# Branch condition loaded once a batch, and other hand-written step orders on five engines, in a 32-batch conditional transformer stack

## The chip, the cores and the metric

The program runs on one core of one Trainium2 chip. The metric is the device time of that core in microseconds (us) for the whole batch of 32 sequences; lower is better.

## What is computed

Each of 32 batch entries is a 256 x 256 matrix of float32 (256 tokens, width 256). It passes four layers.

```python
x = rotate(x, theta[b], phi[b])                      # pairs of columns turned by an angle
h = gelu(x @ Wi[e] + bi[e]); o = h @ Wo[e] + bo[e]   # e = expert of this batch entry, width 1024
x = layernorm(o + x) * gamma[e] + beta[e]
# one of three branches, by c = itok_B_0_2[b]
c == 0: out = gelu(x @ w1_nr + b1) @ w2_nr + b2
c == 1: out = gelu(x @ w1_tsr + b1) @ w2_tsr + b2
c == 2: out = gelu(gelu(x @ w1_sr + b1) @ w2_sr + b2) @ w3_sr + b3      # w1_sr is 256 x 512
x = layernorm(x + out) * gamma + beta
x = layernorm(x) * (1 + scale[b]) + shift[b]          # from a time step
p = softmax(q k^T / 4 + bias[b] + mask[b])            # 16 heads of 16, bias is 16 x 256 x 256 per entry
x = x + (p v) @ Wo
x = x + gelu2(layernorm(x) @ W1) @ W2                 # width 1024
```

In the data of this case c is 0 in 12 of the 32 entries, 1 in 10 and 2 in 10 (entries 2, 4, 8, 10, 11, 15, 17, 18, 27 and 30).

## The kernel before

The kernel is written engine by engine. Each engine has one instruction stream in program order, and the streams meet only through semaphores (`wait_ge`, `then_inc`). The work of a batch entry b is cut into four streams of steps:

- wide, letter g: rotation and expert layer. On TensorE (PE) its steps are the transposes of the input ("turnx0"), wide_in 0 to 3 and wide_out 0 to 3; on VectorE (DVE) `rotate`, then the sum with its statistics, then the scaling of layer 1, called scale1 below; on ScalarE (ACT) the copy of x0 and four gelus.
- front, letter f: the branch, the second and third normalisation, q, k and v. On PE: transposes of y1 ("turny1"), branch_in, branch_middle, branch_out, transposes of x2, q, k, v. On DVE the first step makes x1's low part (xa_lo); scale3 is the third scaling (it makes x2). On ACT the first step makes x1's high part (xa_hi), the second ("br_a") the gelu of the branch, the third seeds PSUM with the branch's bias row ("seedF"), the fourth ("br_b") is the second gelu of c == 2 and only a semaphore step otherwise.
- attention, letter h: for each head h of 16, PE has scores S(h) (a mask matmul and two score matmuls) and T(h) (four transposes of the shifted scores), after every fourth head the values V and the context transposes C (V1 and C1 come with heads 8 and 9, V2 and C2 with heads 12 and 13, V3 and C3 with heads 0 and 1 of the next entry). DVE has the maxima M(h): two additions of the bias with a row maximum, two subtractions. ACT has the exponential E(h). T(h) waits for M(h)'s subtractions and for E(h-1), since there is one PSUM bank of transposed scores; S(h+1) waits for M(h)'s additions.
- tail, letter r: output projection and the feed-forward layer. On PE: transposes, wo, transposes, then the halves "hidden" 0 to 3 (h0 to h3) and "narrowed" 0 to 3 (n0 to n3), 12 matmuls each. On ACT seed, tanh and high for each m2; on DVE x3lo (the low part of the layer's input), gate g0 to g3 and low l0 to l3.

Matrices are split in a high and a low part, so that a product of 256 x 256 is 12 matmuls; branch_in and branch_middle have 24 for c == 2.

The order in which an engine takes the steps of the four streams is a hand-written string of letters: `FIRST[engine] + ORDER[engine] * 25 + LAST[engine]`, where each letter takes the next step of that stream. `ORDER` is one batch entry's worth of steps (68 letters on PE, 48 on ACT, 46 on DVE, 7 on GpSimd, 27 on the DMA queue of SyncE). The streams are offset against each other: while the attention of entry b runs its second half, front works on entry b+2 and wide on entry b+3.

Three places on PE (L597, L608, L619), two on ACT (L847, L859) and two on DVE (L1133, L1141) read the entry's condition c from SBUF into a register with `value_load` and branch on it with `e.If`. In branch_in the load stands behind the wait for `x1_hi`, in branch_out behind the wait for `branch_seeded`, in ACT's br_a behind the waits for `dma_spill`, `wide_out`. The waits for buffers: br_a writes `hid`, which the previous entry's q and k spills (DMAs out of `hid`) must have left.

SyncE issues every DMA in one order. A bias block for head h+7 waits for T(h); the fetch of expert weights (raw0 to raw3) waits for wide_out 0 to 3; the load of the next x waits for scale1's first half; out waits for the end of the tail; the spills wait for q's and k's low parts; st0 and st1 bring the spilled q and k back as stacks. DVE's scale3 waits for the out DMA of two entries earlier (`dma_out`), since `res` has three buffers.

Of the kernel before, what the change touches and what calls it, by code (L numbers as in the profile page):

```python
# [43 lines left out]
    "DVE": (
        "gggffffffgffffghhhghhfhfhghhfhhfhffhhfhfhfhfggfhhfhgfhfhffhfhrhhrfrhfrfhhghrhghrrfhhhrhrfhgfhhrr"
        "hfrhhfhhrrfrhrhrfghfrg"),
    "POOL": "ggffggfffgfggffrrfgfrgfgfr",
    "SP": "gggggfffggfhgghghhhhhhfhghhghfgfgfghhfhhhfhhhhghgffghhhfhgghhfhhhrhfghhhgghhggh",
}
ORDER = {  # L50
    "PE": "hhfhhfhhhhfrrhhfrhhfhhhghhhghhrhhghhhhhhgrgrhhgghhrgghhrfhhhhfrrhhfr",
    "ACT": "rhrhrfhrrhfrrrhfrhfrfhhfhrffrhfhhrhghhghhhgrhghg",
    "DVE": "hrhfrhrfhrhfhhrfhrfhghrhhhrhhfhfrhrhrfhrfghrfg",
    "POOL": "frgrfgf",
    "SP": "hfhfhhfhhhhffggrhhhhhhghghg",
# [3 lines left out]
        "hhhhhhhhfhhrhhrhhhhfhhfrhhfhhgfhhhghhhgrhhrgrghhgrhhhfghrfhhgfhhhhghhfhrfhhhfhhfrfghhrghhhrhhhrg"  # L59
        "rhhghhghhhrhhhrghrhgfghhrfhhhhhhrfhhghhfhhhhhhrrrhhffhhhhrhhhhrhhhhffhhhhhhrhhrrhhhhrhhhhfrhhfhh"  # L60
        "rhhhhhhrfhhrhhrhhhhhhfrhhrhhrhhhhhhrrhhhhrhhhhhhrhhhhrhhhhhhrrhhrhhrhhhhhhrhhrhhhhhhhhhhrrrhhrhr"
        "hhhhrhhhhhrhhhrhrhrhhhhhhhhrhhhhhhr"),
# [4 lines left out]
    "DVE": (
        "hrhfrhhrhfhhrhrhhgfhhrfhhffhfrhhfrhrrrhfrhfhfhhfrhghgrfhhrfghfhrrfhhrhhrhrhfrhhfrfrhrfhrhfhhhfhr"
        "hgrhrhghfrhrhfhhhfrhrfhfhhrhfhrrhrfrhhfrhhrhfrhhrhfhrhhhrhrhrhrhhrhrhrhhrhrhhrhrhhrhrrhhrhhrhhhr"
        "hhrhrrrhhhhrhhhrhrrrhrrhrrrhhhhh"),  # L70
    "POOL": "fgfrrggfffrfgrffrfrrrrr",
# [1301 lines left out]
```

## Time and profile before

| | us |
|---|---|
| median of 3 runs | 2076.05 (2075.35 to 2077.53) |
| span of the profiled execution | 2069.5 |
| PE busy | 1921.3 (93%) |
| weight loads of PE busy | 1676.1 (81%) |
| DVE busy | 1590.7 (77%) |
| ACT busy | 1376.7 (67%) |
| GpSimd busy | 252.4 (12%) |
| DMA, mean over the span | 172 GB/s |

The span goes from the first to the last instruction of one profiled execution. The profile gives no device time of that execution beside it; the median lies 6.55 us above the span. Busy is the time in which an instruction of the engine runs. A matmul's record of 0.28 us starts every 0.12 us when PE runs without a break, so records overlap, and an idle time counts from the end of the last record.

### The profile page before, as it was taken

How to read it: one execution, taken by the hardware profiler on the slowest of the kernel's cores; microseconds unless marked ns; L12 is line 12 of the kernel's file. 1: busy time of each engine (PE TensorE's matmuls, PEld its weight loads, DVE VectorE, ACT ScalarE, POOL GpSimd, SP SyncE). 2: the span in 40 equal slices, each digit the busy share in tenths (PEclk: the TensorE clock that was granted, in tenths of full speed). 3: DMA queues.
4: the chain of work that ended last, by engine and by line, in shares of the span. 5: the costliest groups of instructions: out<-in, count | busy, mean ns of one | idle time of the engine just before them, and what ended most of it. 6: DMA issues, size and time to landing. Idle time of an engine off the chain costs nothing.

```text
span 2069.5 us, 43614 instructions
## 1 busy us (share of the span) xinstructions
PE 1921.3 (93%) x14354; PEld 1676.1 (81%) x14354; DVE 1590.7 (77%) x5373; ACT 1376.7 (67%) x2210; POOL 252.4 (12%) x361
## 2 busy tenths in 40 slices
PE   5789999999999999999999999999999999999786
PEld 4668888888888888888888888888888888788676
DVE  4577877787887788887777888778888877877774
ACT  3376677677667677767767767766776776666443
POOL 1111111011111011111001111101111110111100
PEclk9799999999999999999999999999999999999998
DMA  6655555665565566654555655556665546653450
GB/s 221 202 172 167 187 153 158 186 203 182 183 178 148 156 202 192 196 181 154 154 187 183 195 172 179 164 174 201 189 196 181 177 146 177 216 159 118 133 153 11
DMA packets 222311, 356.12 MB, mean 172 GB/s; under 512 B 29523, under 2 KB 120147, under 8 KB 222068
## 3 DMA queue, kind: packets, MB, share of 16 engines
q1 hardware_dynamic: 222068, 352.99, 56.0%
q8 instruction: 139, 2.28, 0.5%
q14 instruction: 104, 0.85, 0.1%
HBM read 294.12 MB, written 58.79 MB: 171 GB/s over the span
## 4 chain that ended last, share of the span: by engine, by line
PE 76%; DVE 12%; issue 5%; ACT 4%; DMA 1%; ACTq 0%; SPq 0%; POOL 0%; DVEq 0%; POOLq 0%
PE pD L471 51%; PE pX L687 11%; PE pS L471 9%; DVE bias_ring L1178 4%; PE pC L471 3%; DVE bias_ring L975 3%; PE pC L709 1%; DVE x_nat L972 1%; ACT L777 1%; DVE crossed L972 1%; ACT gelu_out L777 1%; ACT probs L777 1%; ACT hid L777 1%; DVE res L978 0%; DVE y_nat L978 0%
## 5 line engine op out<-in xcount | busy, mean ns | idle before, releaser
L1178 DVE CUSTOM_DVE_ANT_0 bias_ring<-pS,bias_ring 128x256 f32<-128x256 f32 x1024 | 389.5, 418 | 200.3 <-PE pS L471 197.4
L777 ACT ACTIVATE probs<-pX 128x512 f32<-128x512 f32 x512 | 304.6, 595 | 225.1 <-PE pX L687 222.8
L777 ACT ACT_TABLE_LOAD x341 | 437.5, 1283 | 18.9 <-PE pD L471 12.0
L687 PE MATMUL pX<-ident,bias_ring 128*128 128x128 f32 x2048 | 321.2, 280 | 61.4 <-DVE bias_ring L975 49.3
L687 PEld LDWEIGHTS pX<-ident,bias_ring 128*128 128x128 f32 x2048 | 228.9, 141 | 147.2 <-issue 95.9
L975 DVE TENSOR_SCALAR bias_ring<-bias_ring,row_max 128x256 f32<-128x256 f32 x1024 | 321.8, 357 | 18.3
L471 PE MATMUL pS<-k_stack,q_stack 96*128 96x256 f32 x1024 | 304.5, 379 | 0.0
L471 PE MATMUL pD<-x,raw 128*128 128x256 f32 x1024 | 246.4, 384 | 3.0 <-ACT gelu_out L777 1.0
L471 PE MATMUL pD<-raw,gelu_out 128*128 128x256 f32 x1024 | 237.6, 379 | 0.0
L471 PEld LDWEIGHTS pS<-k_stack,q_stack 96*128 96x128 f32 x1024 | 197.9, 193 | 19.8
L471 PEld LDWEIGHTS pD<-x,raw 128*128 128x128 f32 x1024 | 188.2, 191 | 31.8 <-issue 9.7
L471 PE MATMUL pD<-w_hi,ffn 128*128 128x256 f32 x1024 | 206.3, 284 | 0.6 <-ACT ffn L777 0.6
L471 PEld LDWEIGHTS pD<-raw,gelu_out 128*128 128x128 f32 x1024 | 187.3, 190 | 22.2 <-issue 0.4
L471 PE MATMUL pS<-mask_add,eye_bf 128*128 128x512 bf16 x512 | 196.0, 383 | 0.9 <-DMA k_stack<-k_spill 0.9
L471 PEld LDWEIGHTS pD<-w_hi,ffn 128*128 128x128 f32 x1024 | 168.5, 191 | 1.8 <-issue 0.8
L1264 POOL TENSOR_SCALAR front_var_eps<-front_mean_var 128x2 f32<-128x2 f32 x64 | 13.3, 207 | 1240.8 <-DVE front_mean_var L1059 1198.1
L777 ACT ACTIVATE gated<-pD 128x512 f32<-128x512 f32 x128 | 76.4, 597 | 109.0 <-PE pD L471 109.0
L777 ACT ACTIVATE gelu_out<-pD,chosen 128x256 f32<-128x256 f32 x300 | 126.0, 471 | 33.4 <-PE pD L471 31.8
L471 PE MATMUL pD<-xc_hi,w_hi 128*128 128x256 f32 x512 | 131.6, 289 | 6.1 <-ACT pD L777 6.1
L471 PE MATMUL pC<-probs,v_aug 128*17 128x256 f32 x2048 | 135.4, 382 | 0.7 <-issue 0.7
L471 PE MATMUL pD<-xc_hi,w_lo 128*128 128x256 f32 x512 | 130.0, 286 | 0.0
L471 PE MATMUL pD<-w_lo,ffn 128*128 128x256 f32 x512 | 128.4, 283 | 0.0
(148 smaller groups left out, 3663.4 us busy)
## 6 DMA issues: line engine op xcount, KB each, us to landing
bias_ring<-in_fside SPq DMA_DIRECT2D x512, 256.0 KB, 4.4
raw<-in_experts SPq DMA_DIRECT2D x128, 512.0 KB, 4.7
q_spill<-hid SPq DMA_DIRECT2D x96, 256.0 KB, 3.4
k_spill<-hid SPq DMA_DIRECT2D x96, 256.0 KB, 3.4
q_stack<-q_spill SPq DMA_DIRECT2D x128, 192.0 KB, 4.3
k_stack<-k_spill SPq DMA_DIRECT2D x64, 384.0 KB, 5.6
norm<-in_expert_rows SPq DMA_DIRECT2D x32, 384.0 KB, 4.1
x_nat<-in_x SPq DMA_DIRECT2D x32, 256.0 KB, 3.1
```

The source lines that it names most:

```text
L471: return e.matmul(o, lhsT, rhs, start=start, stop=stop, skip_group_check=True, **kw)
L687: last = e.transpose(pX[:, k, t * P:(t + 1) * P], bias_ring[:, u % NBIAS, t, k * P:(k + 1) * P], ident[:, :])
L709: last = e.transpose(pC[:, 1, t * P:(t + 1) * P], ctx_raw[:, t * P:(t + 1) * P], ident[:, :])
L777: return e.activation(o, i, func, bias=bias, scale=scale)
L972: return e.tensor_tensor(o, a, c, op)
L975: return e.tensor_scalar(o, a, s1, None, op0) if op1 is None else e.tensor_scalar(o, a, s1, s2, op0, op1)
L1178: e.tensor_tensor_reduce(bias_ring[:, n, t, :], pS[:, t, :], bias_ring[:, n, t, :], 1.0, -3.4e38, ALU.add, ALU.max, row_max[:, n, t:t + 1] ...
L1264: e.tensor_scalar(var_eps[which][:, :], mean_var[which][:, :, 1], eps, 1.0, ALU.add, ALU.mult).then_inc(sem[which + "_eps"], 1)
```

## The change

The condition is loaded once at the start of the front stream's first step of a batch entry on PE, ACT and DVE, in front of that step's waits, and the register serves all branches of that entry. The waits that stood ahead of the branches now stand inside each arm. The three strings of every engine are replaced.

In the cyclic part this makes the following moves. PE: V1 goes in front of turny1; n1 goes from behind branch_in to between T9 and S10, so that the order is T8 S9 V1 turny1 T9 n1 S10 C1 branch_in h3 T10 S11 branch_middle n2 T11 S12 branch_out (before: T8 S9 turny1 V1 T9 S10 C1 branch_in n1 h3 T10 S11 branch_middle n2 T11 S12 branch_out). The rest of PE's cycle is as before. ACT: E6 in front of seed2 and high1, mask in front of seed3, tanh3 and E10 in front of seedF, C2's copy in front of high3. DVE: rotate goes from between M12 and M13 to between M9 and xa_lo, l2 in front of M10, g3 from behind M11 to between M12 and M13, klo in front of l1, l0 in front of the normalising of context 0, scale3 in front of x3lo. GpSimd: the root of the third normalisation (root3) goes in front of two additions, of which one comes last now. SyncE: st0 one bias block later, st1 two earlier, then raw0, out, block 14, raw1, block 15, raw2, block 0, raw3, x and norm1, blocks 1 and 2, q spill (before: raw0, raw1, out, blocks 14 to 3, raw2, block 4, raw3, block 5, x and norm1, block 6, q spill); so blocks 3 to 7 come between the q spill and the k spill, where before only block 7 did. Block h here is the one that waits for T(h). FIRST and LAST hold the same moves for the entries at the ends and some swaps of neighbours.

```diff
--- before.py
+++ after.py
...
 ORDER = {
-    "PE": "hhfhhfhhhhfrrhhfrhhfhhhghhhghhrhhghhhhhhgrgrhhgghhrgghhrfhhhhfrrhhfr",
-    "ACT": "rhrhrfhrrhfrrrhfrhfrfhhfhrffrhfhhrhghhghhhgrhghg",
-    "DVE": "hrhfrhrfhrhfhhrfhrfhghrhhhrhhfhfrhrhrfhrfghrfg",
-    "POOL": "frgrfgf",
-    "SP": "hfhfhhfhhhhffggrhhhhhhghghg",
+    "PE": "fhhhfhrhhfrhhfrhhfhhhghhhghhrhhghhhhhhgrgrhhgghhrgghhrfhhhhfrrhhfrhh",
+    "ACT": "fhrrhfrhrrfrhffrhhfhrfrhffhhhrghhghhhgrhghgrhrhr",
+    "DVE": "frhfrhrhgfhrhfhfhrhrhhhrhhfhfrhrhrfhfrghrfgrhh",
+    "POOL": "frfggfr",
+    "SP": "hfhhhfhfhfhgrhghghgghhfhhhh",
 }
...
@@ -592,20 +592,20 @@
             def front(b):
                 def branch_in():
                     xa = [(xa_hi[:, k, :], xa_lo[:, k, :]) for k in range(K)]
-                    low = sem["x1_lo"], b + 1
-                    e.wait_ge(sem["x1_hi"], b + 1)
-                    c = e.value_load(idx[0:1, 1, b:b + 1])
+                    high, low = (sem["x1_hi"], b + 1), (sem["x1_lo"], b + 1)
                     with e.If(c == 2):
+                        e.wait_ge(*high)
                         for i in range(2):
                             to_turned(BANK[f"deep{i}"], "w1_sr", SR, 2 * P * i, xa, low).then_inc(sem["pe_deep"], 1)
                     with e.Else():
                         with e.If(c == 1):
+                            e.wait_ge(*high)
                             to_turned(BANK["narrow"], "w1_tsr", H, 0, xa, low).then_inc(sem["pe_narrow"], 1)
                         with e.Else():
+                            e.wait_ge(*high)
                             to_turned(BANK["narrow"], "w1_nr", H, 0, xa, low).then_inc(sem["pe_narrow"], 1)
 
                 def branch_middle():
-                    c = e.value_load(idx[0:1, 1, b:b + 1])
                     with e.If(c == 2):
                         e.wait_ge(sem["dve_deep"], 3 * b + 2)
                         ins = [(hid[:, s, 0, n, :], hid[:, s, 1, n, :]) for s in range(2) for n in range(2)]
@@ -615,20 +615,26 @@
 
                 def branch_out():
                     ins = [(hid[:, 0, 0, n, :], hid[:, 0, 1, n, :]) for n in range(2)]
-                    e.wait_ge(sem["branch_seeded"], b + 1)
-                    c = e.value_load(idx[0:1, 1, b:b + 1])
+
+                    def narrow_ready():
+                        e.wait_ge(sem["branch_seeded"], b + 1)
+                        e.wait_ge(sem["act_narrow"], 3 * b + 3)
+                        e.wait_ge(sem["dve_narrow"], b + 1)
+
                     with e.If(c == 2):
+                        e.wait_ge(sem["branch_seeded"], b + 1)
                         e.wait_ge(sem["act_deep"], 9 * b + 9)
                         to_natural(SUM_F, "w3_sr", 0, ins, (sem["dve_deep"], 3 * b + 3), start=False).then_inc(sem["branch_done"], 1)
                         e.sem_inc(sem["pe_narrow"], 1)
                     with e.Else():
-                        e.wait_ge(sem["act_narrow"], 3 * b + 3)
-                        e.wait_ge(sem["dve_narrow"], b + 1)
                         with e.If(c == 1):
+                            narrow_ready()
                             to_natural(SUM_F, "w2_tsr", 0, ins, start=False).then_inc(sem["branch_done"], 1)
                         with e.Else():
+                            narrow_ready()
                             to_natural(SUM_F, "w2_nr", 0, ins, start=False).then_inc(sem["branch_done"], 1)
 
+                c = e.value_load(idx[0:1, 1, b:b + 1])
                 if b:
                     e.wait_ge(sem["v_made"], 2 * b)
                 e.wait_ge(sem["y1_made"], b + 1)
@@ -834,21 +840,25 @@
                     e.wait_ge(sem["pe_deep"], 3 * b + i + 1)
                     gelu_and_hi(BANK[f"deep{i}"], i % 2, i % 2, [col(name, first + n) for n in range(2)], "act_deep", 9 * b + 3 * i)
 
+                c = e.value_load(idx[0:1, 1, b:b + 1])
                 e.wait_ge(sem["y1_turned"], b + 1)
                 if b:
                     e.wait_ge(sem["branch_done"], b)
                 act(flat(xa_hi[:, :, :]), flat(pD[:, BANK["y1"], :, :]), ACT.Copy).then_inc(sem["x1_hi"], 1)
                 yield
-                if b:
-                    e.wait_ge(sem["dma_spill"], 96 * b)
-                e.wait_ge(sem["wide_out"], 4 * b + 4)
-                if not b:
-                    e.wait_ge(sem["dve_cols"], 1)
-                c = e.value_load(idx[0:1, 1, b:b + 1])
+                def hid_free():
+                    if b:
+                        e.wait_ge(sem["dma_spill"], 96 * b)
+                    e.wait_ge(sem["wide_out"], 4 * b + 4)
+                    if not b:
+                        e.wait_ge(sem["dve_cols"], 1)
+
                 with e.If(c == 2):
+                    hid_free()
                     deep(0)
                     deep(1)
                 with e.Else():
+                    hid_free()
                     narrow()
                 yield
 
@@ -856,7 +866,6 @@
                 e.wait_ge(sem["dma_brow"], 16 * (b + 1))
                 act(pD[:, SUM_F, :, :], branch_row[:, :].unsqueeze(1).to_broadcast([P, T, H]), ACT.Copy).then_inc(sem["branch_seeded"], 1)
                 yield
-                c = e.value_load(idx[0:1, 1, b:b + 1])
                 with e.If(c == 2):
                     e.wait_ge(sem["dve_deep"], 3 * b + 1)
                     deep(2)
@@ -1119,6 +1128,7 @@
                 yield
 
             def front(b):
+                c = e.value_load(idx[0:1, 1, b:b + 1])
                 e.wait_ge(sem["x1_hi"], b + 1)
                 low_of(xa_hi[:, :, :], xa_lo[:, :, :], flat(pD[:, BANK["y1"], :, :])).then_inc(sem["x1_lo"], 1)
                 yield
@@ -1130,7 +1140,6 @@
                     e.wait_ge(sem["act_deep"], 9 * b + 3 * i + 3)
                     low_part(i % 2, i % 2, "dve_deep")
 
-                c = e.value_load(idx[0:1, 1, b:b + 1])
                 with e.If(c == 2):
                     deep(0)
                     deep(1)
@@ -1138,7 +1147,6 @@
                     e.wait_ge(sem["act_narrow"], 3 * b + 3)
                     low_part(0, 0, "dve_narrow")
                 yield
-                c = e.value_load(idx[0:1, 1, b:b + 1])
                 with e.If(c == 2):
                     deep(2)
                     e.sem_inc(sem["dve_narrow"], 1)
```

The changed strings of FIRST and LAST are left out where the diff shows "...".

## Rows read from the trace of the kernel before

**Rows 1.** The page: DMA issues, KB each, median us from issue to landing.

```profile
bias_ring<-in_fside SPq DMA_DIRECT2D x512, 256.0 KB, 4.4
```

**Rows 2.** Busy time by stretch: start, middle, end, one cycle (stretch, length, busy).

```profile
0.00:277.70 277.70, 228.67 (x1493) 195.59 (x1493) 181.49 (x563) 156.99 (x254) 33.79 (x50) 0.93 0.61 185
277.70:1739.90 1462.20, 1411.41 (x10716) 1235.64 (x10716) 1172.59 (x3999) 1042.25 (x1658) 185.80 (x264) 1.00 0.59 179
1739.90:2069.50 329.60, 281.26 (x2146) 244.83 (x2146) 236.60 (x813) 177.44 (x300) 32.83 (x47) 0.96 0.43 130
827.40:886.90 59.50, 57.46 (x437) 50.30 (x438) 48.52 (x168) 42.27 (x68) 7.74 (x11) 1.00 0.61 184
```

**Rows 3.** Waits of PE: line, waited for; total us, times, longest.

```profile
PE pX L687 <- DVE bias_ring L975: 49.3, 85, 2.1
PE pD L471 <- DVE x_nat L972: 20.3, 20, 13.3
PE pD L471 <- issue: 18.4, 31, 4.1
```

**Rows 4.** Chain that ended last, in order of time: start, us, what.

```profile
813.74 0.59 issue
814.33 4.58 PE pD L471 x36
```

**Rows 5.** Lines 597 and 598 on PE's sequencer: ns min/median/max.

```profile
L597 PEldq TENSOR_LOAD <-idx x32: 296/302/497, 38.3 to 1918.8; - x32
L598 PEldq COMPARE_BRANCH  x42: 68/207/361, 38.8 to 1919.2; - x42
```

**Rows 6.** Timeline of ACT, 812.8 to 819 us: start, us, instruction, [idle before].

```profile
812.82 0.59 ACT L777 ACTIVATE xa_hi<-pD 128x512 fp32r<-128x512 f32 x1
...
814.43 1.28 ACT L777 ACT_TABLE_LOAD   x1
...
818.93 0.60 ACT L777 ACTIVATE gated<-pD 128x512 f32<-128x512 f32 x1 [0.89 <-PE pD L471]
```

**Rows 7.** Timeline of PE: the breaks at T11, turnx0, T13; branch_out of a c == 2.

```profile
821.49 0.66 PE L687 MATMUL pX<-ident,bias_ring 128*128 128x128 f32 x4 [0.28 <-ACT probs L777]
826.34 0.63 PE L471 MATMUL pD<-ident,x_nat 128*128 128x128 f32 x4 [0.17 <-DVE x_nat L972]
827.42 0.63 PE L687 MATMUL pX<-ident,bias_ring 128*128 128x128 f32 x4 [0.45 <-DVE bias_ring L975]
...
1069.38 0.39 PE L471 MATMUL pD<-w_hi,hid 128*128 128x256 f32 x1 [0.60 <-ACT hid L777]
```

**Rows 8.** Timeline of DVE: xa_lo, the rotation's first and last instruction.

```profile
813.44 0.69 DVE L972 TENSOR_TENSOR xa_lo<-pD,xa_hi 128x512 fp32r<-128x512 f32 x1 [0.93 <-ACT xa_hi L777]
...
823.98 0.76 DVE L972 TENSOR_TENSOR crossed<-x_nat,rot_sin 128x256 f32<-128x256 f32 x2
...
825.50 0.69 DVE L972 TENSOR_TENSOR x_nat<-x_nat,crossed 128x512 f32<-128x512 f32 x1
```

**Rows 9.** Timeline of DVE: x3lo, scale3 behind it, and M8.

```profile
851.86 0.68 DVE L972 TENSOR_TENSOR xc_lo<-pD,xc_hi 128x512 fp32r<-128x512 f32 x1
852.78 0.88 DVE L978 SCALAR_TENSOR_TENSOR res<-y_nat,front_mean_var,norm 128x256 f32<-128x256 f32 x2 [0.23 <-issue]
...
868.22 0.42 DVE L1178 CUSTOM_DVE_ANT_0 bias_ring<-pS,bias_ring 128x256 f32<-128x256 f32 x1 [0.44 <-PE pS L471]
```

**Rows 10.** Timeline of PE: the first matmul of h0.

```profile
854.90 0.28 PE L471 MATMUL pD<-xc_hi,w_hi 128*128 128x256 f32 x1
```

**Rows 11.** DMA issues on SyncE's queue: k spills, the next stack load, norm1.

```profile
808.58 1.54 SPq L294 DMA_DIRECT2D k_spill<-hid  x3
...
813.52 0.86 SPq L294 DMA_DIRECT2D q_stack<-q_spill  x2
...
860.69 0.34 SPq L294 DMA_DIRECT2D norm<-in_expert_rows  x1
```

**Rows 12.** DMA view, 840 to 904 us in 40 slices: GB/s moved.

```profile
GB/s 0 13 271 47 0 72 255 392 403 408 401 351 188 259 159 41 326 291 216 342 149 149 360 239 128 161 56 108 164 0 159 5 67 258 257 117 13 0 0 238
```

More of the change, by code:

```diff
@@ L37 @@
     "PE": (
-        "gggggggggffffgffgfgfgggggghhhhhhfhhhhhfhhhfhhhghhfhhghhhghhhgghhfgfhhgghhfghfhhfhfhhfhhfghhhghhh"
-        "ggfrghhghhrghhfrgfhhhhgrhhfhhrhhhfhhhfrhhrhhrhhhfhhhrgfhhgrhhghhhghhhrrghrhgghhrgghhrfhhhhfrrhhf"
-        "r"),
+        "gggggggggffffgffgfggggfggghhhhhhfhhhhhfhhhfhhhghhfhhghhhghhhgghhfgfhhgghhfghhfhfhfhhfhhfghhhghhh"
+        "ggfrghhghhrghhhfrgfhhhgrhhfhhrhhhfhhhfrhhrhhrhhfhhhhrgfhhghrhghhhghhhrrghrhgghhrgghhrfhhhhfrrhhf"
+        "rhh"),
     "ACT": (
-        "gggggffffgffgfgggffhhhhfhffhhfhghhghhghhfgfhghfhfhfffhffhghhgghrhgfhgfrhrfhhrhfrhrrfhhfhrfhrfhrh"
-        "hrfrhrghrghghhhrhgg"),
+        "gggggffffgffgfgggffhhhhfhffhhfhghhghhghfhgfhghfhffhffhffhghhgghrhgfhgfrhfhrhhrfrhrhfrfhhrfhrfhrr"
+        "fhhrhrghrghhghhrhggrhrhr"),
     "DVE": (
[L45 to L48, printed above, removed]
+        "gggffffffgffffghhhghhfhfhghfhhhfhffhhfhfhfhfgghfhfhgfhffhfhfhhrhrfrfrhfhhghrhghrrfhhhrhrfhgfhhrr"
+        "hfhrhfhhrfrrhrhrfghfrgrhh"),
+    "POOL": "ggfffggfffggffrgfgrfrgffgr",
+    "SP": "gggggffgfgghfhghghhhfhghhfhgfgghhhfghhfhfhhhhhhgghfgfgghfhhhhfhhrhhhfhghgghhgghhf",
 }
 ORDER = {
-    "PE": "hhfhhfhhhhfrrhhfrhhfhhhghhhghhrhhghhhhhhgrgrhhgghhrgghhrfhhhhfrrhhfr",
-    "ACT": "rhrhrfhrrhfrrrhfrhfrfhhfhrffrhfhhrhghhghhhgrhghg",
-    "DVE": "hrhfrhrfhrhfhhrfhrfhghrhhhrhhfhfrhrhrfhrfghrfg",
-    "POOL": "frgrfgf",
-    "SP": "hfhfhhfhhhhffggrhhhhhhghghg",
+    "PE": "fhhhfhrhhfrhhfrhhfhhhghhhghhrhhghhhhhhgrgrhhgghhrgghhrfhhhhfrrhhfrhh",
[3 more added lines that the diff above has]
+    "SP": "hfhhhfhfhfhgrhghghgghhfhhhh",
 }
@@ L58 @@
     "PE": (
[L59 to L62, printed above, removed]
+        "hhhhhhfhhrhhrhhhhfhhfrhhfhhgfhhhghhhrghhrgrghhgrhhhfghrfhhgfhhhhghhfhrfhhhfhhfrfghhrghhhrhhrhgrh"
+        "hghhghhhrhhhrhrghgfghhrfhhhhhhrfhhghhfhhhhhhrrrhhffhhhhhrhhhrhhhhffhhhhhhrhhrhhrhhrhhhhfrhhfhhrh"
+        "hhhhhrfhhrhhrhhhhhhfrhhrhhrhhhhhhrrhhhhrhhhhhhrhhhhrhhhhhhrrhhrhhrhhhhhhrhhrhhhhhhhrhrhhhrrhrhhr"
+        "hhhhhhhhhhhrrhrhrhhhhhhhhrhhhhhhr"),
     "ACT": (
-        "rhrrhfhrrfrhrrhhhfhrhrhfrhfhhrhffhffhrghhghgrhhghrhrfhrfghfrhrfhfhrfhfrffhgrhrhgrhhrgrhrhhghhrhf"
-        "hrfhrhghfhrhrhhrffrhrrfrhhfhrhhfhrfhrhrhhhrhhhfhrhrhfrhhrrhrfrhhrhrhhfrfhrhrhrhhhrhhhhrrhhrhrrhh"
-        "rrhrrrhrhhhrhhhrhhhrrrhhhrrrrrhhrhrhhrhhhhrrhhrhh"),
+        "fhrrfrhrrhhhfhhrrhfrhfhhrfhfffhrhghhghrghghhrhrfhrfghfhrrffhrhfhfrfrfhghrhgrhhrrghhrhghhrhfhrfhr"
+        "hghfhrhhrhrhffrrrfrhhfhrhfhhrhfrrhhhhhrhhfhrhrhrfhhrrhrrfhhrhrhhffrrhhrhrhhhrhhhhrhrhrhrrhhrrhrr"
+        "rhrhhhrhhhrhrhrhhhrhrrrhrrhrrhrhhrhhhrrhhhhh"),
     "DVE": (
[L68 to L71, printed above, removed]
+        "frhhrhfhhrhhrhgfhhrfhfhfhfrhhfrhrrrhfrhffhhrhfhghgrfhhrfghfhrhrfhrhhrhrhfrhhfrfrhrfhrhfhhhfhrhgh"
+        "rrhghfrhrhfhhhrfhfrhfhhrhfhrrhrfrhhfrhhrhfrhhrhfhrhhhrhrhrhrhhrhrhrhhrhrhhrhrhhrhrrhhrhhrhhhrhrh"
+        "rhrrhhrrhhhhhrhhrrrrhrrrhhhhh"),
+    "POOL": "gffrgfgrffrrfgffrrrrfrr",
     "SP": (
-        "hfhhfhhhhfhfhhfhhghrhhghgfhfhghghfhffhhhhrhhhhffhhhhhhhhhhffhfhhrghhhhhhhhgffhfhhhhfhhghhhhghhhh"
-        "hhhhhhhhhhhhhhrfrhhhhhhhhhrghh"),
+        "hhfhfhhhhhfhfhrhhhhghghfhgfhgghfhffhhhhrhhhhhhffhhhhhfhhhfhhhfhrghhhhhhhgffhfhhfhhhghhhhhghhhhhh"
+        "hhhhhhhhhhhhrfrhhhhhhhrhhghh"),
 }
```

## The prediction

> **What bounds the kernel now.** I read the busy times by stretch first. In the middle, where the cycle of orders runs, PE is busy 1411.41 of 1462.20 us; in the first 277.7 us and the last 329.6 us it idles 49.0 and 48.3 us [rows 2]. One cycle of a c below 2 is 59.50 us with PE busy 57.46, DVE 48.52, ACT 42.27 and DMA at 0.61 [rows 2]. So PE bounds the cycle, at full clock (1.00), and only what closes a break on PE can shorten it. The reader is to see how little there is: 2.04 us a cycle. The waits of PE then say who makes the breaks: the subtractions of DVE 49.3 us, the rotated x_nat 20.3 us (13.3 of it once, at the start), and 18.4 us of "issue", 31 times, once an entry [rows 3]. The chain of waits shows the last kind in front of branch_in: 0.59 us in which nothing but PE's own sequencer is late, then 36 matmuls in 4.58 us, which is 1.5 us for each group of 12 [rows 4].
>
> PE's records overlap when it runs unbroken: 0.28 us each, one every 0.12 us. A break of r us in the records therefore costs about r + 0.14 us. That is 0.73 in front of branch_in, 0.42 at T11, 0.31 at turnx0, 0.59 at T13 [rows 4, 7].
>
> **The change, part by part (a cycle with c below 2).**
>
> Load of c, and branch_in. Before, xa_hi is written until 812.82 + 0.59 = 813.41; only then does the sequencer load c (0.30 us) and branch (0.07 to 0.36 us), and the first matmul starts at 813.74 + 0.59 = 814.33 [rows 4 to 6]. So 0.92 us pass between the data and the work. After, n1 (1.44 us at 0.12 a matmul), S10 and C1 lie between turny1 and branch_in. xa_hi needs turny1, ACT's copy of context 1, and its own 0.59 us, so by my count it is there about 1 us before branch_in's turn; the branches run while PE works off what is queued. I leave 0.1 us of the 0.73. Gain 0.63. n1's cover is not lost elsewhere: it is the same work in another place, and l1 and high1, which it needs, come before M9 and E7 in both orders. The load itself (0.30) moves to turny1, behind V1's matmuls (about 1 us of work); if that cover went, it would cost its 0.30.
>
> T11. It waits for E10, E10 for a table load of 1.28 us behind tanh3, and tanh3 for h3 [rows 6, 7]. Between h3 and T11 PE does T10, S11, n2 in both orders, and tanh3 starts right behind h3 in both. The 0.42 stays; gain 0. br_a's gelus and copy and h3 (1.44) now run side by side and end together, which may push tanh3 by 0 to 0.1. SeedF, a copy of xa_hi's size (0.59 us), now stands behind E10 and holds the table load of E11 back by that much; by my count E11 ends at T12's turn, so the cost is between 0 and 0.3; I take 0 to 0.1.
>
> turnx0 and T13. The rotation is 825.50 + 0.69 - 823.98 = 2.21 us on DVE [rows 8]. It stood between M12 and M13: turnx0 waited for it, and T13 for M13 behind it [rows 7]. Now it stands behind M9, where DVE idled 0.93 us [rows 8], and only g3 precedes M13, 0.68 us as x3lo, which has its size [rows 9]. x is there: its load goes out ahead of norm1's at 860.69 [rows 11], and M9 follows M8 of 868.22 [rows 9]. M13 then starts when S13 is done, and V2 and turnx0 cover its two additions of 0.42 us [rows 9] and the first subtraction. Gain 0.31 + 0.59 = 0.9, of which 0 to 0.1 may stay at T13. What is late next: xa_lo comes 1.3 us later against xa_hi, but branch_in needs it only after 8 of its matmuls (0.96 us) and starts later against turny1 by n1; by the rows 0.6 us are to spare. M10, with l2 (0.7, again of x3lo's size) now ahead of it, has 0.3 us to spare before T10. If both were gone, each 0.1 us more would be 0.1 us a cycle.
>
> scale3 in front of x3lo. x3lo ran 851.86 to 852.54, and scale3 started at 852.78 [rows 9]; its wait for the out DMA ended then, since out was issued behind raw1. After, out is issued some 5 us earlier and scale3 starts at once. x3lo gets 1.8 us later (scale3 1.80), to about 854.2; seed0 (0.60) follows, to 854.9, and h0's turn is at 854.90 [rows 10]. Cost 0.1 (0 to 0.4).
>
> DVE's, ACT's and GpSimd's other swaps (klo and l1, E6 and seed2, mask and seed3, l0, root3, C2's copy and high3) move steps of under 1.5 us inside stretches in which PE waits for none of them: 0.
>
> Sum: 0.63 + 0.9 = 1.53 without any cost, and 1.53 - 0.1 (T13) - 0.1 (T12) - 0.1 (h0) = 1.23 with them. I take 1.35: the 0.1 at h0 I count, of the other two half.
>
> A cycle with c == 2: the break in front of branch_in is only 0.2 in the records, turnx0 and T13 are as above, and branch_out's 0.60 stays, because it hangs on the end of branch_middle, a table load and a gelu in both orders [rows 7]. Gain 0.25 + 1.0 - 0.1 = 1.15.
>
> Places: the new order holds for the front steps of entries 4 to 28, 17 of them with c below 2 and 8 with c == 2: 17 x 1.35 + 8 x 1.15 = 32. In a third of the entries the branch takes the long 0.33 us instead of 0.2 [rows 5]; that goes too: 2. Ends: 97 us of idle [rows 2], of which the swaps touch little; some branch_in breaks there go too. I take 3, between -4 and 8. Total 37 us: 2069.5 becomes 2032.5 in the profiled execution, and with the 6.55 us that the median stands above the span, 2039.
>
> **SyncE's queue and the DMAs.** Before, the k spills are issued from 808.58 and have landed by 813.52, when the stack load that waits for them goes out [rows 11]. br_a waits for them too, and its table load of 1.28 us comes behind that wait; the table load started at 814.43, high2 and not the spill deciding [rows 6]. After, blocks 3 to 7 (5 x 256 KB) stand between q and k spill. Issue takes 0.5 us each and fits into the time up to k's low part; on the DMA engines, 1.3 MB at 400 GB/s, which the DMA view shows where blocks follow each other [rows 12], is 3.3 us, of which about 2.5 falls into idle time of the engines or the wait for k. branch_in ends 0.7 us later against k's step than before, so the spill may land 1.2 us later and cost nothing. I take 0.
>
> The Trainium skill, DMA: Bandwidth & Descriptors (Queues, rings and completion order), says that each DMA engine takes the descriptors of a ring in ring order, so the spill would stand behind all five blocks; taken alone it speaks for the second rival below.
>
> **The rivals.**
> - The sequencer stays exposed. The gain at branch_in is only the load, 0.37 us, and a first branch of 0.2 to 0.36 still shows [rows 5]. For it: the branch decides what is fetched next, so nothing of the arm can be queued before. Against: in c == 2 the load and a 0.07 us branch leave 0.2. Loses 0.35 x 25 = 9: 2048. The Trainium skill, Runtime: NRT & Kernel Launch (Instruction fetch mechanics), says that a taken branch out of the fetched window stalls on a fetch; that speaks for this rival.
> - The k spill lands late, more than 1.2 us behind its time: at 2.2 us more, branch_a's gelu, tanh3, E10 and T11 shift by 1 us. 25 x 1 = 25: 2064.
> - Slower: x and norm1 now stand ahead of block 1 and wait for scale1; norm1 goes out at 860.69, block 1 at about 861.2, and M8 starts at 868.22 [rows 9, 11]. Landing takes 4.4 us as a median [rows 1], so 2.6 of 7.0 us are free. Above 7.0 + 1.35 = 8.35 us the lateness outweighs the gain. At 9.5 us: (2.5 - 1.35) x 25 = 29 more, less the 5 of the ends and long branches: 2100. It decides from a mean landing of twice the median.
> - The gains of one break are eaten by the next (xa_lo behind the rotation, M10, E11): DVE has 0.3 us to spare at M10; 1.3 us lost there a cycle gives about 2073.
>
> **How the numbers follow.** Forecast 0.55 (own range 2028 to 2050), exposed sequencer 0.17, late spill 0.15, gains eaten 0.07, slower 0.06. All of the cycle's breaks but T11 gone and 8 us at the ends would be 2028; the late spill is the upper end, 2064. That leaves 0.13 above and little below. A measurement of this kernel tells 0.2% (4 us) from no change. Faster by more: 0.88; within: 0.06; slower: 0.06.
>
> **What would show it.** Right: PE's waits lose x_nat (20.3 to about 14, the start's 13.3 staying) and most of "issue"; DVE's subtractions fall from 49.3 by 25 x 0.45 = 11; the cycle is 58.1 us for c below 2; the 0.28 at T11 and 0.60 at branch_out stay. Exposed sequencer: "issue" still 0.2 or more in front of branch_in. Late spill: ACT's table load of br_a starts behind the spill, and T11's break grows. Slower: M(8) or M(9) waits for bias_ring from DMA. The prediction is wrong if DVE or ACT becomes continuous between T8 and T13, or if the ends grow.

## The result and the profile after

The changed kernel takes 2112.0 us (median, 2108.5 to 2117.0) against 2075.35 us of the kernel before on the same chip: ratio 1.0185, 95% interval 1.0170 to 1.0199 (as recorded for all runs; the two medians alone would give 1.0177). It is slower by 1.9%, where 2039 was forecast. The profiled execution spans 2110.3 us, 40.8 more than before; the medians differ by 36.7. The table below splits the 40.8 of these two executions, so a place in it can be off by a few us: the runs of the kernel before lie between 2070.6 and 2077.5.

The longest waits of PE in the changed kernel (what PE waited for, us in total, times, longest one), to be held against [rows 3]:

```profile
engine line waited for: us in total, times, longest us
PE pX L693 <- ACT probs L783: 39.0, 27, 3.5
PE pX L693 <- DVE bias_ring L984: 35.4, 61, 1.4
PE pD L471 <- ACT pD L783: 22.7, 32, 3.1
PE pD L471 <- DVE hid L981: 15.9, 10, 2.7
PE pD L471 <- DVE x_nat L981: 13.6, 2, 13.3
PE pD L471 <- ACT hid L783: 7.6, 10, 1.8
PE pD L471 <- DVE ffn_in L1086: 5.3, 3, 3.7
PE pS L471 <- DMA k_stack<-k_spill: 5.0, 1, 5.0
PE pD L471 <- issue: 5.0, 15, 0.5
```

What the change was to remove did go: "issue" (PE waits for nothing that the profile shows) 18.4 to 5.0, the rotated x_nat 20.3 to 13.6, the subtractions of DVE 49.3 to 35.4 (11 was forecast, 14 came). Of the 15 "issue" breaks 14 stand in front of turny1, behind the moved load of c, and none in front of branch_in. In place of what went stand waits for ACT, for the exponentials (probs) and for the seed of the tail's bank (pD), and 5 us once for the k stack.

To see where they fall I measured the cycle from start to start of PE's steps (first weight load of each, in one traced execution of each kernel): means over the 17 entries with c below 2 among the entries 5 to 28 of the front stream, in us. The last three rows are sums over all entries. "All four" is the best kernel of the experiments below; each column right of it has one of its four edits undone.

| c below 2 | before | changed | all four | waits in arms | GpSimd | x3lo | SyncE |
|---|---|---|---|---|---|---|---|
| T8 to branch_in | 4.37 | 5.22 | 4.97 | 4.98 | 4.98 | 4.98 | 5.04 |
| branch_in to T11 | 7.17 | 7.05 | 5.74 | **7.05** | 5.73 | 5.74 | **6.08** |
| T11 to T13 | 5.89 | 4.87 | 4.86 | 4.86 | 4.86 | 4.86 | 4.87 |
| T13 to T4 | 26.41 | 26.44 | 26.44 | 26.44 | 26.44 | 26.44 | 26.44 |
| T4 to T5 (h0) | 4.05 | 4.82 | 4.11 | 4.11 | 4.12 | **5.25** | 4.09 |
| T5 to T6 | 5.46 | 5.72 | 5.43 | 5.46 | **6.33** | 5.38 | 5.41 |
| T6 to T8 | 6.24 | 6.33 | 6.24 | 6.24 | **6.33** | 6.24 | 6.24 |
| cycle | 59.59 | 60.45 | 57.79 | 59.14 | 58.79 | 58.89 | 58.17 |
| start, up to T8 of entry 2 | 255.5 | 267.0 | 253.3 | 262.2 | 258.8 | 255.5 | 264.0 |
| 24 cycles | 1467.0 | 1492.4 | 1429.5 | 1461.3 | 1453.1 | 1456.1 | 1435.9 |
| end | 347.0 | 350.9 | 343.5 | 351.7 | 347.4 | 345.0 | 345.1 |

So of the 40.8 us, 11.5 are lost in the start, 25.4 in the 24 cycles and 3.9 at the end. In the cycle the move of n1 puts 1.44 us of work ahead of branch_in and takes it from branch_in to T11, so 7.17 ought to become 5.73; it is 7.05. That is the largest loss, and h0 (0.77) and T6 (0.26) are the others. The rotation's gain, T11 to T13, is there in full (1.02).

ACT and PE at that place in the changed kernel, entry 14 of the front stream, c = 0 (start, duration, what; in brackets the idle time before it and what ended it), to be held against [rows 6, 7]:

```profile
898.46 1.28 ACT L783 ACT_TABLE_LOAD   x1 [2.24 <-PE pD L471]
899.75 0.84 ACT L783 ACTIVATE gelu_out<-pD,chosen 128x256 f32<-128x256 f32 x2
900.62 0.63 ACT L783 ACTIVATE hid<-gelu_out 128x512 fp32r<-128x512 f32 x1
901.16 0.58 ACT L783 ACTIVATE gated<-pD 128x512 f32<-128x512 f32 x1
901.76 1.28 ACT L783 ACT_TABLE_LOAD   x1
903.05 0.60 ACT L783 ACTIVATE probs<-pX 128x512 f32<-128x512 f32 x1
...
903.70 0.66 PE L693 MATMUL pX<-ident,bias_ring 128*128 128x128 f32 x4 [1.59 <-ACT probs L783]
```

The gelu's table load now waits for the branch's own matmuls, which end at 898.35; before, it ran while they ran. From it to T11 ACT is a closed chain: table load, gelus, copy, tanh3, table load, E10, and PE's break is 1.59 where it was 0.28.

### The profile page after: what moved, and what is told of

Read it like the earlier page. It is cut to its first block, busy times and chain, and to the rows that moved or that the text cites. A ratio compares the mean times of both kernels' runs of the same rounds, so it can differ in the third digit from the quotient of the medians.

```text
span 2110.3 us, 43295 instructions
## 1 busy us (share of the span) xinstructions
PE 1935.4 (92%) x14130; PEld 1687.3 (80%) x14354; DVE 1611.2 (76%) x5373; ACT 1370.7 (65%) x2209; POOL 242.8 (12%) x361
## 3 DMA queue, kind: packets, MB, share of 16 engines
HBM read 294.12 MB, written 58.79 MB: 167 GB/s over the span
## 4 chain that ended last, share of the span: by engine, by line
PE 72%; DVE 11%; ACT 10%; issue 5%; DMA 1%; SPq 0%; POOL 0%; ACTq 0%; DVEq 0%; POOLq 0%
PE pD L471 46%; PE pX L693 11%; PE pS L471 9%; ACT L783 4%; PE pC L471 4%; DVE bias_ring L1186 3%; ACT gelu_out L783 2%; DVE bias_ring L984 2%; DVE res L987 2%; PE pC L715 1%; ACT probs L783 1%; ACT pD L783 1%; DVE xc_lo L981 1%; ACT gated L783 1%; ACT hid L783 1%
## 5 line engine op out<-in xcount | busy, mean ns | idle before, releaser
L984 DVE TENSOR_SCALAR bias_ring<-bias_ring,row_max 128x256 f32<-128x256 f32 x1024 | 339.0, 373 | 18.3
L471 PEld LDWEIGHTS pD<-xc_hi,w_hi 128*128 128x128 f32 x512 | 99.2, 194 | 25.7 <-DVE xc_lo L981 18.8
```

Of the source, the lines that this page charges most:

```text
L471: return e.matmul(o, lhsT, rhs, start=start, stop=stop, skip_group_check=True, **kw)
L984: return e.tensor_scalar(o, a, s1, None, op0) if op1 is None else e.tensor_scalar(o, a, s1, s2, op0, op1)
```

## The experiments

All ratios are to the kernel before, measured on the same chip, with 95% intervals. The times of steps are read from one traced execution of each kernel, as in the table.

**1. ACT's waits ahead of its If.** The three waits (k spill landed, wide_out, and for the first entry the columns) stand outside the arms again, as before the change; the hoisted load stays.

```diff
+                hid_free()
                 with e.If(c == 2):
-                    hid_free()
                     deep(0)
                     deep(1)
                 with e.Else():
-                    hid_free()
                     narrow()
```

> The changed kernel with one edit: ScalarE's waits for dma_spill and wide_out stand ahead of the branch again, so that each arm begins with the wait for the matmuls alone. Theory 1 (the table load of 1.28 us in front of the branch's gelu was pushed behind the end of branch_in by those waits): the load runs during branch_in again, the break in front of T11 falls from about 1.6 to 0.3 us, 1.3 us less in each of 25 cycles: about 33 us less than the changed kernel, 2079 us. Theory 2 (the k spill lands late behind five bias blocks and holds the gelu): the gelu still waits, the time stays within 5 us of 2112. Theory 3 (vector engine held by GpSimd's additions around M4 and scale1): the same, 2112, since those breaks are elsewhere.

Measured: 2088.61 us, 1.0076 (1.0053 to 1.0100). That is theory 1, with 23 us of its 33: branch_in to T11 is 5.74 us at best, but 6.45 on the mean and 7.29 at worst, since ACT now waits 41.8 us in all for the k spill.

**2. GpSimd's strings of before** in the changed kernel (`ORDER` "frgrfgf" for "frfggfr": the addition for the next entry's input stands again between root4 and the tail's addition, ahead of root3; `FIRST` and `LAST` likewise).

> The changed kernel with GpSimd's three strings of the kernel before. Theory 3 (GpSimd's addition of 1.3 us now runs beside M4's first subtraction, which then takes 0.98 instead of 0.36 us, and another one beside scale1's first instruction, 1.46 instead of 0.48): both durations go back to the short ones, h0 comes 0.6 and T6 0.3 to 0.4 us earlier a cycle, so 20 to 25 us less, 2088 us; the norm step gets its 0.8 us more again, without a cost on TensorE. Theory 1 alone (only the table load matters): no change, 2112.

Measured: 2086.02 us, 1.0061 (1.0042 to 1.0079), 26 us less than the change; theory 3. T4 to T5 is 4.40, T5 to T6 5.38.

**3. Both.**

> Both edits together. If theories 1 and 3 each own a separate break, the gains add: 2112 - 33 - 22 = 2057 us, about 18 us below the kernel before. If one hides the other, no less than 2075.

Measured: 2053.75 us, 0.9903 (0.9878 to 0.9927). This already beats the kernel before, and the two edits give 58 us together against 23 and 26 alone. Part of it lies at T11, where the late spill costs less in this kernel (5.94 from branch_in to T11, against 6.45 in experiment 1).

**4. The strings alone**, with the code of before (each branch loads c itself, behind its waits).

> The kernel before with all the strings of the changed one and none of its other edits, so three loads of the condition as before. Theory 1: the table load is free, since the load of the condition stands between the waits and the arm; only branch_in's load of the condition (0.3 to 0.4 us, with n1 ahead of it now mostly hidden) is left: 2080 us, like the kernel with the wait ahead, up to 5 us more. If the strings and not the code carry the loss: 2105 to 2112.

Measured: 2115.18 us, 1.0220 (1.0176 to 1.0263). The strings alone cost as much as the whole change: the second expectation, 3 us above its range. So the waits in the arms are not the only way to this loss. ACT waits for the spill, 3.14 us in entry 14, and its load of c and the table load stand behind that wait; and branch_out, whose load of c stands behind the wait for the seed, takes 5.79 us from T11 to T13 in the mean (5.23 to 8.34) against 4.87. T8 to branch_in is 4.97, the same as with all four edits: with n1 ahead of branch_in the load costs nothing at its old place there, and what loading c once buys beside the new strings lies at branch_out.

```profile
898.88 1.28 ACT L777 ACT_TABLE_LOAD   x1 [3.14 <-DMA k_spill<-hid]
...
904.13 0.66 PE L687 MATMUL pX<-ident,bias_ring 128*128 128x128 f32 x4 [2.19 <-ACT probs L777]
```

**5. The code alone**, with every string of before.

> The changed code with every order string of the kernel before. Theory A (the arm's three waits, now one group in front of ACT's table load, cost more than the hoisted loads give): ACT's gelu of the branch starts about a table load (1.28 us) after the branch's matmuls instead of 0.3 us, T11 comes 0.5 to 1.3 us later a cycle in the 17 cycles with c below 2, the loads give back 0.3 to 0.8 us a cycle: 2080 us (2070 to 2090). Theory B (the steps of the prediction, by which the waits' new place costs nothing and each hoisted load is a gain of 0.3 to 0.4 us where it was exposed): 17 x 0.8 + 8 x 0.6 = 18 us less than the kernel before, about 2057 us. The two are told apart by the idle time of ACT ahead of the branch's first gelu and by the interval from the branch's first matmuls to T11.

Measured: 2078.05 us, 1.0019 (1.0010 to 1.0029). T8 to branch_in falls from 4.37 to 3.87, so the hoisted load gives 0.50 us; branch_in to T11 grows from 7.17 to 7.56 by the merged waits. The two cancel. Theory A held. That the waits in the arms cost only 0.39 us here and 1.31 in experiment 9 follows from the rows of before: there ACT idled 0.89 us ahead of tanh3, waiting for h3 [rows 6], and 1.28 for the table load less 0.89 is 0.39. With n1 out of the way h3 ends 1.44 us earlier, and tanh3 starts in "all four" 0.04 us behind it (859.49 and 859.45): no idle time is left to take the table load.

**6. SyncE's strings of before too**, on top of the third.

> The changed kernel with ACT's waits on hid ahead of its If and GpSimd's strings of before (that one took 2053.75 us), and now SyncE's strings of before too. Theory A (the k spill stands behind bias blocks 3 to 7 in the changed SyncE string and so holds back the branch's first gelu in part of the cycles, and the first batch's raw0 ahead of the stack transfer costs some us at the start): the spill lands 3.4 us after its issue again, T11 follows the branch's matmuls by 5.7 us in nearly all cycles with c below 2, 0.4 us x 24 less in the middle and 3 us less at the start: about 2041 us (2036 to 2046). Theory B (the later spill is covered and the rest is lost elsewhere, in the register loads and in VectorE's order): 2052 us (2050 to 2055).

Measured: 2058.27 us, 0.9920 (0.9904 to 0.9937). Both theories missed. branch_in to T11 is 5.74 in every entry with c below 2, as theory A wanted, and the start is 255.5 (262.6 in the third kernel); but T4 to T5 went from 4.40 to 5.25. The timelines of DVE, ACT and SyncE there:

```profile
1029.44 0.62 DVE L983 TENSOR_SCALAR bias_ring<-bias_ring,row_max 128x256 f32<-128x256 f32 x2
1030.72 0.88 DVE L986 SCALAR_TENSOR_TENSOR res<-y_nat,front_mean_var,norm 128x256 f32<-128x256 f32 x2 [0.66 <-issue]
1031.64 0.88 DVE L986 SCALAR_TENSOR_TENSOR res<-res,front_rstd,norm 128x256 f32<-128x256 f32 x2
1032.55 0.69 DVE L980 TENSOR_TENSOR xc_lo<-pD,xc_hi 128x512 fp32r<-128x512 f32 x1
...
1033.28 0.60 ACT L783 ACTIVATE pD<-cols 128x512 f32<-128x512 f32 x1 [1.90 <-DVE xc_lo L980]
...
1026.32 0.43 SPq L294 DMA_DIRECT2D out<-res  x1
```

scale3 writes the res buffer that the out transfer of three entries ago (not two, as said in the description of the kernel) must have left. That transfer is issued at 1026.32, behind raw1, and takes 4.4 us in the median (next fence): 1030.72, when scale3 starts. x3lo stands behind scale3, and seed0, which overwrites what x3lo reads, behind x3lo. With SyncE's changed string it goes out 9.5 us ahead of T4 in the mean (third kernel) instead of 5.6, about 4 us earlier in the cycle, and scale3 does not wait.

```profile
out<-res SPq DMA_DIRECT2D x32, 256.0 KB, 4.4
```

**7. x3lo ahead of scale3 again** in DVE's cyclic string, on top of the sixth. With this all four edits are in: "all four" in the table.

```diff
-    "DVE": "...fhfrghrfgrhh",      # h M4, f scale3, r x3lo, g sum1
+    "DVE": "...fhrfghrfgrhh",      # h M4, r x3lo, f scale3, g sum1
```

> The kernel with SyncE's strings of before, and one pair exchanged in VectorE's cyclic string: x3lo stands again ahead of scale3, as before the change. Theory A (h0 starts late because its low half waits for scale3 in front of it, 0.23 to 0.8 us a cycle): h0's break shrinks by that and T5 comes 0.2 to 0.4 us earlier a cycle, 5 to 10 us less than the kernel without the exchange: about 2034 us. Theory B (M4 and x3hi set h0's start, scale3 is covered): no difference, within 2 us of that kernel.

Measured: 2030.56 us, 0.9788 (0.9772 to 0.9805), the best kernel of this study, 2.1% faster than before. The step was worth 27.7 us, not the 5 to 10 of theory A: I had taken scale3's duration and not its wait for the out transfer. T11 in it:

```profile
855.88 1.28 ACT L783 ACT_TABLE_LOAD   x1
858.05 0.84 ACT L783 ACTIVATE gelu_out<-pD,chosen 128x256 f32<-128x256 f32 x2 [0.89 <-PE pD L471]
...
862.05 0.66 PE L693 MATMUL pX<-ident,bias_ring 128*128 128x128 f32 x4 [0.28 <-ACT probs L783]
```

**8. The register load later**, on top of the seventh: behind the four matmuls of turny1 on PE, behind x1hi on ACT, behind x1lo on DVE.

> As the kernel with x3lo ahead of scale3, but the register load of c stands on TensorE behind the four matmuls of turny1, on ScalarE behind the eviction x1hi and on VectorE behind x1lo, instead of ahead of their waits. Theory A (a register load takes 0.3 to 1.3 us while SyncE's transfers and the other engines' loads run, and ahead of turny1 it is not covered, so turny1 is 0.1 to 0.5 us late in many cycles): behind turny1 the queued matmuls and the wait for x1hi cover it; turny1 comes on time, 0.1 to 0.3 us less a cycle, 3 to 7 us less. Theory B (the loads are already covered by the waits behind them, and turny1 waits for its data in any case): no difference, or up to 5 us more, where the load now delays T9 behind it.

Measured: 2029.39 us, 0.9780 (0.9761 to 0.9800). 1.2 us less than the seventh, which cannot be told from no difference; theory B.

**9. All four, with the waits in the arms again.**

> The best kernel so far (2030.56 us: ACT's waits on hid ahead of its If, GpSimd's and SyncE's strings of before, x3lo ahead of scale3 in VectorE's cycle) with the first of these four undone: ACT's waits on hid stand inside the arms again, as in the change. Theory A (inside the arm they are merged with the wait for the branch's matmuls into one group ahead of the table load, whatever else is on time): T11 comes 1.3 us later a cycle with c below 2 and 1.6 us later with c == 2, 17 x 1.3 + 8 x 1.6 = 35 us more: 2065 us (2056 to 2070). Theory B (the merged waits only hurt with the late spill; with the spill on time only the 0.4 to 0.5 us remain that the code alone showed with the old strings): 2042 us (2036 to 2046).

Measured: 2078.65 us, 1.0026 (1.0011 to 1.0040): 48 us more than with all four, above the range of theory A. In the 24 cycles it is 31.8 us, close to theory A's 35 (1.31 us at T11 for c below 2, 1.32 for c == 2); the start and the end lose 8.9 and 8.2 us more, which it had left out. The spill is on time here (landed 3.5 us after its issue, and ACT has no wait for it), so the placement alone does it:

```profile
880.46 1.28 ACT L783 ACT_TABLE_LOAD   x1 [2.34 <-PE pD L471]
...
885.70 0.66 PE L693 MATMUL pX<-ident,bias_ring 128*128 128x128 f32 x4 [1.59 <-ACT probs L783]
```

**10. All four, with GpSimd's changed strings.**

> The best kernel so far (2030.56 us) with GpSimd's three strings of the change. Theory A (GpSimd's 128x512 additions then run beside M4 and scale1 and stretch them, 0.35 to 0.98 us and 0.48 to 1.46 us, which comes out at T5 and T6 by 0.3 to 0.8 us a cycle): 25 x 0.5 = 13 us more, 2043 us (2037 to 2050). Theory B (GpSimd's order hurt only through x3lo behind scale3, which now stands ahead of it): within 3 us of 2030.6.

Measured: 2061.08 us, 0.9939 (0.9918 to 0.9961): 30.5 us more; theory A's cause, with twice its size. DVE and GpSimd ahead of T6, with y_nat's instructions on DVE in that stretch (ns min/median/max), then the same view of "all four":

```profile
1029.33 1.24 DVE L983 TENSOR_SCALAR bias_ring<-bias_ring,row_max 128x256 f32<-128x256 f32 x2
...
1028.89 1.27 POOL L1277 TENSOR_TENSOR x_nat<-x_nat,norm 128x512 f32<-128x512 f32 x1
...
1037.03 1.95 DVE L986 SCALAR_TENSOR_TENSOR y_nat<-x_nat,wide_mean_var,norm 128x256 f32<-128x256 f32 x2
...
1037.02 1.28 POOL L1277 TENSOR_TENSOR res<-res,ff_row 128x512 f32<-128x512 f32 x1
...
L986 DVE SCALAR_TENSOR_TENSOR y_nat<-x_nat,wide_mean_var,norm x2: 474/1013/1552, 1037.0 to 1038.5; 128x256 f32<-128x256 f32 x2
...
1042.35 0.63 PE L693 MATMUL pX<-ident,bias_ring 128*128 128x128 f32 x4 [0.55 <-DVE bias_ring L983]
```

```profile
1019.67 0.87 DVE L986 SCALAR_TENSOR_TENSOR y_nat<-x_nat,wide_mean_var,norm 128x256 f32<-128x256 f32 x2
...
L986 DVE SCALAR_TENSOR_TENSOR y_nat<-x_nat,wide_mean_var,norm x2: 474/476/479, 1019.7 to 1020.1; 128x256 f32<-128x256 f32 x2
```

An instruction of DVE of 0.48 us that starts beside GpSimd's addition lasts 1.55 us, until 0.28 us after the addition has ended; M4's subtractions take 1.24 instead of 0.62. With GpSimd's old string one of these additions falls beside the normalisation of the tail (two instructions in 1.68 us instead of 0.73); of those 0.95 us, 0.64 fall into time in which DVE otherwise idles ahead of M4. With the new string both fall between M4 and M6, where DVE has no idle time, and add 0.62 + 1.08 = 1.70 us. 1.70 less the 0.31 saved ahead is 1.39; 0.99 arrives at PE; that the rest was slack at T6 is an inference.

**11. All four, with SyncE's changed strings.**

> The best kernel so far (2030.56 us) with SyncE's three strings of the change. Theory A (the k spill stands behind blocks 3 to 7 and lands 1 to 3 us later, so that the branch's gelu waits for it in part of the cycles; the first batch's raw0 ahead of the stack transfer costs 3 us at the start; the register loads on TensorE lengthen beside this traffic): 0.45 x 24 + 3 = 14 us more, 2044 us (2038 to 2051). Theory B (the later spill is covered, only the start counts): 2034 us (2032 to 2037).

Measured: 2046.40 us, 0.9869 (0.9852 to 0.9886): 16 us more, theory A in its size but not in its places: 6.4 in the 24 cycles and 10.7 in the start (in the traced executions, whose spans differ by 18.7). SyncE's issues, ACT's table load, and the landing times of this kernel, and below them the landing with all four:

```profile
860.64 2.99 SPq L294 DMA_DIRECT2D bias_ring<-in_fside  x5
863.67 2.54 SPq L294 DMA_DIRECT2D k_spill<-hid  x3
...
870.91 1.28 ACT L783 ACT_TABLE_LOAD   x1 [1.09 <-DMA k_spill<-hid]
...
ACT L783 <- DMA k_spill<-hid: 32.3, 25, 2.6
...
k_spill<-hid SPq DMA_DIRECT2D x96, 256.0 KB, 5.1
```

```profile
k_spill<-hid SPq DMA_DIRECT2D x96, 256.0 KB, 3.4
```

**12. The changed kernel with x3lo ahead of scale3, and nothing else.**

> The changed kernel with nothing but x3lo put back ahead of scale3 in VectorE's cyclic string. Theory A (x3lo behind scale3 is the whole of h0's lateness, 0.76 us a cycle): 19 us less than the changed kernel's 2112, about 2093 us (2088 to 2098). Theory B (with GpSimd's strings of the change M4's stretched subtraction holds x3lo back just as much): 5 us less, about 2107 us.

Measured: 2110.16 us, 1.0177 (1.0159 to 1.0195), 2 us less than the change: near theory B's number, but by another way. T4 to T5 falls to 4.12, the full 0.70; T5 to T6 grows from 5.72 to 6.39 and takes it back. DVE runs without a break from M4 to M6 (M4's subtractions 1.25 us, scale1's first pair 1.95 here too), and the order within it only says which of PE's steps meets its lateness.

## Why the prediction was wrong, step by step

The forecast was 37 us faster, and the change is 37 us slower. The forecast gains are real: with all four edits, which take back GpSimd's and SyncE's strings, the kernel takes 2030.6 us, 8 below the forecast of 2039, and a cycle with c below 2 gains 1.80 us, where 1.35 was forecast. The sum of the changes is wrong in the costs that were set at nothing.

- *Load of c and branch_in (0.63), T11 (0).* With all four, T8 to T11 takes 10.71 instead of 11.54: 0.83, and 0.28 stays in front of T11, as said. The gain at branch_in would have come from n1 alone: experiment 4 has the load at its old place and the same 4.97. In the changed kernel T8 to T11 takes 12.27. The step that failed is "between h3 and T11 [...] tanh3 starts right behind h3 in both". In the changed kernel tanh3 starts 1.36 us behind the end of h3 (901.16 and 899.80). I looked at the order of steps and not at what moved inside br_a: its waits went into the arms, in front of the first gelu together with the wait for branch_in's matmuls, and the table load of 1.28 us, which had been covered by those matmuls, now follows that wait. Experiment 9 has this as its only difference: 1.31 of the 1.56 us. The other 0.25 is turny1, late behind the load of c, a cost that the prediction had named (0.30, if V1's cover went) and set at 0.
- *turnx0 and T13 (0.9).* Right; 1.02 measured, in every kernel with the new strings of PE and DVE and the load ahead (0.10 in experiment 4, where branch_out's load takes the rest).
- *scale3 in front of x3lo (0.1, between 0 and 0.4).* With the out transfer early and GpSimd's old string it is 0.35 (experiment 3), inside the bounds, but at their upper end. In the changed kernel it is 0.77: GpSimd's addition stretches M4's subtractions ahead of it from 0.62 to 1.25. I had rightly named the wait for the out transfer; experiment 6 shows what it costs where that transfer is late (1.2 us).
- *GpSimd's swaps ("inside stretches in which PE waits for none of them: 0").* The step that failed most plainly. I counted steps of under 1.5 us on GpSimd, for which nobody waits, and not what they do to DVE beside them: 0.99 us a cycle from T5 to T8 in experiment 10, 30.5 us in all. The trace of before had the rows for it, the tail's normalisation stretched beside the same addition (1.68 us, and 0.73 in experiment 10 where nothing runs beside it), and I did not read them as such:

```profile
848.01 1.68 DVE L1077 TENSOR_SCALAR ffn_in<-res,tail_mean_var,tail_rstd 128x256 f32<-128x256 f32 x2
...
847.79 1.42 POOL L1270 TENSOR_TENSOR x_nat<-x_nat,norm 128x512 f32<-128x512 f32 x1
```

  The Trainium skill, SBUF — State Buffer (Who interferes with whom), has the rule: a VectorE instruction with two SBUF inputs, beside a GpSimd instruction that reads SBUF, or one in a two-port mode, which tensor_scalar can enter, contends with GpSimd for a shared port pair, and whoever comes second is blocked until the first has finished. This case's trace agrees in the main: 1.55 us instead of 0.48, ending 0.28 us behind GpSimd's instruction. A full block and then 0.48 us would have ended 0.2 us later still; GpSimd's spans in a trace are rough.
- *SyncE's queue (0).* The second rival, the late spill, was right in kind: landing 5.1 us instead of 3.4, and the wait shows as soon as the table load no longer hides it (up to 7.24 us from branch_in to T11 in experiment 11). SyncE's strings cost 6.4 us in the cycles there, 0.34 at T11 for c below 2, not the rival's 1 us a cycle or 25; in experiment 1, with GpSimd's changed strings, it is 0.71 at T11. In the changed kernel itself the late spill is hidden behind the wait for the matmuls (branch_in to T11 is 7.04 to 7.05 in all 17 entries), so it is not what made its cycles long. The Trainium skill, DMA: Bandwidth & Descriptors (Queues, rings and completion order), which the prediction weighed for this rival, has the descriptors of a ring consumed in ring order; the later landing behind five blocks agrees with it.
- *Sequencer exposed.* Refuted at branch_in, where no "issue" break is left. The 5.0 us in 15 places are almost all at turny1. *Slower by norm1 ahead of block 1.* The sign came, but not by this mechanism: the waits of DVE, which takes the bias blocks, hold none for their transfer in the changed kernel.
- *c == 2 (1.15).* With all four the cycle goes from 64.18 to 63.09, 1.09. In the changed kernel it is 65.64.
- *Ends (a gain of 3, between -4 and 8).* Wrong: the start loses 11.5 us and the end 3.9. Undone one at a time, the waits cost 8.9, GpSimd's strings 5.5 and SyncE's 10.7 us in the start, much more than in one cycle; one 5.0 us wait for the k stack is among them, 1.3 us with all four. What else is in the 11.5 was not taken apart.
- *The sum itself.* The long branch in a third of the entries is 25 / 3 x 0.13, 1 us and not 2; c == 2 takes 1.0 for turnx0 and T13 where 0.9 was worked out. Neither matters. The 6.55 us that the median stood above the span are mostly the difference between executions: the changed kernel's profiled execution took 2112.11 us at a span of 2110.3, so the time is 1.8 us above the span.

Leaving out one of the four edits costs 48.1, 30.5, 27.7 and 15.8 us, 122 together, but the changed kernel is only 81 above the best. They cover one another: the spill's lateness lies behind the wait for the matmuls, and beside GpSimd's changed strings x3lo's place decides only where DVE's lateness comes out.

The range (2028 to 2064) took one cost at a time. What was likely to go wrong were several small ones, each in a resource that the rows of PE do not show.

## What to carry to other kernels

When waits move into the arms of a branch, look at what stands between them and the first activation: a table load behind the wait for the data cost its full duration here (1.3 us a cycle) as soon as the engine had no idle time behind it, and ahead of that wait it cost nothing. When GpSimd's work moves in time, price it by the VectorE instructions that will then run beside it, not by who waits for GpSimd. And when two steps are exchanged because both have slack, check that the transfer which frees the first one's buffer moves with them.

## What the runs showed of the hardware

- A register load is not of fixed length. PE's load of c takes 302/870/1332 ns (min/median/max) in the changed kernel, 300/318/868 with all four edits, and 296/302/497 at its old place in branch_in [rows 5]:

```profile
L637 PEldq TENSOR_LOAD <-idx x32: 302/870/1332, 32.2 to 1958.4; - x32
```

  turny1 and with it branch_in are 0.25 us late in the mean. What sets the length was not shown. At the start of the front step SyncE's changed strings go with the longest loads (medians 727 to 870 ns in the changed kernel and experiments 1, 2, 3, 11 and 12), but with SyncE's strings of before the median goes from 318 in "all four" to 580 in experiment 8, and in experiment 4, with SyncE's changed strings and the load at its old place, it is 307. Experiment 8 shows that with all four edits the place of the load makes no difference to the time.

- In the start the losses show in the granted clock of PE too. It is 0.84 and 0.74 in two stretches of experiment 9 where, with all four, it is 0.99 and 1.00 (the column before the last two); the two kernels differ in nothing but the waits in the arms. PE was busy 5.63 us of the first 10 against 6.44. Experiment 9, then all four (us, busy times of PE, weight loads, DVE, ACT, GpSimd, clock, DMA share, GB/s):

```profile
100.00:110.00 10.00, 5.63 (x41) 4.12 (x40) 5.74 (x20) 7.78 (x11) 0.00 (x0) 0.84 0.18 55
110.00:120.00 10.00, 9.94 (x58) 8.66 (x61) 5.64 (x25) 4.99 (x8) 0.92 (x2) 0.74 0.37 107
```

```profile
100.00:110.00 10.00, 6.44 (x54) 5.03 (x55) 7.31 (x26) 7.03 (x11) 0.00 (x0) 0.99 0.27 79
110.00:120.00 10.00, 10.00 (x67) 8.33 (x67) 8.73 (x34) 8.88 (x12) 2.64 (x5) 1.00 0.31 87
```

  A number between 0.5 and 1 is a stretch in which both levels, 1.2 and 2.4 GHz, occur. How much of the 8.9 us that experiment 9 loses in the start is the clock and how much the waits was not measured.
